# Attention on 128, 128 and 69 rows, angles computed once, both layer norms in one chain: one change to a fused vision-text layer on Trainium2

## What is computed

```python
h = tokens(x) @ W + b + pos          # 1 class token + 196 patches of 3x14x14
h = concatenate([h, txt], axis=1)    # 197 + 128 = 325 rows
xn = layernorm(h)
kp, qp = tanh(xn @ Wk + bk) * pi, tanh(xn @ Wq + bq) * pi     # 4 sets x 8 planes = 32 columns each
V = xn @ Wv + bv
total = sum_s w_s * Re(cumsum(exp(i kp_s) * V) * conj(exp(i qp_s)))   # causal, no softmax
pos = sigmoid(pw) * the same with fixed position angles
g = sigmoid(xn @ Wg + bg)
h = h + xn + (g * total + (1 - g) * pos) / sqrt(8 * position) @ Wo + bo
x2 = layernorm(h)
scores = sigmoid(x2 @ gate.T); top 2 of 64 experts, at most 256 rows each
h = h + shared_ffn(x2) + routed_experts(x2)
```

## Time and profile before

| | us |
|---|---|
| three runs, median (lowest to highest) | 1717.03 (1716.64 to 1719.13) |
| the profiled execution, its own time | 1715.9 |
| its span, first to last instruction | 1714.0 |
| PE busy (share) | 1519.8 (89%) |
| DVE busy | 1470.9 (86%) |
| POOL busy | 1273.1 (74%) |
| ACT busy | 1187.7 (69%) |

### The profile page before, as it was taken

The page is one execution under the profiler, slowest core; times in us unless marked ns, Lnnn a source line. Parts: engine busy times, 40 slices in busy tenths (PEclk is TensorE's granted clock), DMA queues, the critical chain, the costliest instruction groups (busy, mean ns, idle before and its releaser), DMA issues.

```text
span 1714.0 us, 31340 instructions
## 1 busy us (share of the span) xinstructions
PE 1519.8 (89%) x9222; PEld 1169.7 (68%) x9222; DVE 1470.9 (86%) x6005; ACT 1187.7 (69%) x1997; POOL 1273.1 (74%) x1162
## 2 busy tenths in 40 slices
PE   2699999999999999999999999999999981776661
PEld 1477777777777777777777777777777760555551
DVE  2489999999999999999999999999999982886671
ACT  2898888888888888888888888888888740111110
POOL 0018777777777777787777777777777776688888
PEclk9899999999999999999999999999999986898885
DMA  8886666666666666665656566555555111576653
GB/s 132 216 218 140 142 140 137 132 131 124 124 118 120 112 119 112 113 111 110 110 110 111 113 112 110 112 113 113 114 113 111 42 25 45 99 114 89 101 78 34
DMA packets 259939, 193.51 MB, mean 113 GB/s; under 512 B 65514, under 2 KB 239269, under 8 KB 259785
## 3 DMA queue, kind: packets, MB, share of 16 engines
q1 hardware_dynamic: 206008, 173.23, 49.7%
q0 software_dynamic: 51200, 17.87, 8.7%
q10 hardware_dynamic: 2576, 0.60, 0.3%
HBM read 84.34 MB, written 83.73 MB: 98 GB/s over the span
## 4 chain that ended last, share of the span: by engine, by line
PE 72%; POOL 15%; issue 6%; ACT 3%; DVE 2%; DMA 1%; ACTq 1%; SPq 0%; POOLq 0%
PE bank L855 11%; POOL out_rows L602 10%; PE bank L915 8%; PE bank L932 8%; PE bank L1002 5%; PE bank L879 4%; PE bank L1010 4%; PE bank L892 4%; PE bank L863 4%; POOL slot_rows L561 3%; PE bank L974 3%; PE bank L969 2%; PE bank L964 2%; PE bank L986 2%; PE bank L953 2%
## 5 line engine op out<-in xcount | busy, mean ns | idle before, releaser
L561 POOL DMA_INDIRECT slot_rows<-xs,slot x768 | 869.3, 1132 | 241.2 <-issue 240.9
L619 ACT ACTIVATE img<-img 84x980 f32<-84x980 f32 (+1 forms) x192 | 342.2, 1784 | 17.5 <-DVE wcol L1203 13.1
L855 PE MATMUL bank<-img,w_tok 126*128 126x392 f32 (+1 forms) x640 | 224.2, 497 | 11.1 <-DMA img<-img 11.0
L602 POOL DMA_INDIRECT out_rows<-img,etok x128 | 199.5, 1559 | 30.0 <-issue 29.2
L855 PEld LDWEIGHTS bank<-img,w_tok 126*128 126x128 f32 (+1 forms) x640 | 122.9, 192 | 95.2 <-issue 14.7
L688 ACT ACTIVATE xs<-h,nb,rs 128x128 f32<-128x128 f32 x384 | 154.7, 482 | 18.4 <-DVE nb L1257 11.2
L915 PE MATMUL bank<-pos_a,v 128*128 128x325 f32 (+2 forms) x768 | 158.7, 355 | 1.3 <-ACT gt L758 1.3
L701 ACT ACTIVATE xh<-h,nb,rs 128x128 f32<-128x128 f32 x384 | 154.0, 482 | 1.0 <-DVE nb L1230 0.9
L932 PE MATMUL bank<-a_t,v 128*128 128x325 f32 (+2 forms) x768 | 152.0, 346 | 0.0
L539 POOL TENSOR_TENSOR rs<-ve,neg_half 128x6 f32<-128x6 f32 x64 | 87.3, 1365 | 81.2 <-DVE ve L1225 81.1
L915 PEld LDWEIGHTS bank<-pos_a,v 128*128 128x128 f32 (+1 forms) x768 | 125.1, 190 | 30.5 <-ACT gt L758 1.7
(11 more groups left out here) (203 smaller groups left out, 3711.0 us busy)
## 6 DMA issues: line engine op xcount, KB each, us to landing
img<-in_x SPq DMA_DIRECT2D x384, 150.1 KB
img<-img SPq DMA_DIRECT2D x256, 160.8 KB
img<-img SPq DMA_DIRECT2D x128, 128.6 KB
out_rows<-fin SPq DMA_DIRECT2D x128, 128.0 KB
slot_rows<-xs,slot POOLq DMA_INDIRECT x768
slot_rows<-init_rows SPq DMA_DIRECT2D x16, 540.0 KB, 9.5
img<-slot_rows SPq DMA_DIRECT2D x32, 270.0 KB
h<-in_txt SPq DMA_DIRECT2D x64, 128.0 KB, 2.2
```

What stands on the lines that cost most here:

```text
L561: g.indirect_dma_start(out=slots_d, out_offset=bass.IndirectOffsetOnAxis(ap=slot[0:nt, q.x, r, part:part + 1], axis=0), in_=xs[0:nt, q.x, ...
L602: g.indirect_dma_start(out=out, out_offset=bass.IndirectOffsetOnAxis(ap=etok[:, q.load, m:m + 1], axis=0), in_=ysum[:, q.load, m, :], in_o ...
L619: a.activation(cols[:, b0:b0 + nb, :], raw[:, q.u, :].rearrange("p (t b) -> p b t", b=P)[:, b0:b0 + nb, :], ACT.Copy)\
L855: ins = mm(bank[:, 7, 0:2 * PATCHES], w_tok[r, m, :], xk[r, k.u, :, m, :], start=(m == 0), stop=(m == SHIFT - 1))
```

## The change

It redraws the order of every engine's turn and changes four pieces of work.

- **Blocks.** The keys are cut at 128 and 256 instead of 128 and 197 (blocks of 128, 128 and 69 keys, the last from the rows of the third tile of values), so masks and products run over 325 + 197 + 69 = 591 columns a sample in place of 650. `mask` is two operations of 325 and 266 columns in place of one of 650.
- **Angles.** `wkq` has 64 distinct columns; both samples' angles go to one PSUM bank, side by side in its partitions, by two products of 325 columns. One tanh of 325 replaces two, the distance is made with two constants (one for keys, one for queries), and `weighted_queries` writes `qz` in one operation. What ACT moved across partitions is now moved by four DMAs of 32 x 325 on SP (`move_halves`), issued when ACT's `weighted_queries` is done, and `scores` waits for them.
- **One chain.** The statistics of the first norm of pair k and the second norm of pair k-2 lie side by side; one chain of 12 columns and one power on POOL (`rstd`) serve both.
- **Turns.** PE's and DVE's turns reach back to pair k-5, POOL's to k-6, ACT's to k-4, so PE has 69 turns in place of 67. SP spreads piece 1 of pair k+1 (not k+2) and loads pair k+3 (not k+4). During start-up four DMAs of 540 KB that clear `slot_rows` come between `spread_0` and `spread_1`.

The core of the diff (renamed buffers, banks and constants, the DVE body, and repeated forms are left out):

```diff
+BELOW = [L - i * TILE for i in range(NT)]
+BEGIN = [sum(BELOW[0:i]) for i in range(NT + 1)]
...
-    m1 = (p + TILE <= q1) & (p < T1)
-    q2 = np.arange(NIMG, L)[None, :]
-    m2 = p + NIMG <= q2
+    m1 = p + TILE <= q1
+    q2 = np.arange(2 * TILE, L)[None, :]
+    m2 = (p + NIMG <= q2) & (p + NIMG >= 2 * TILE)
...
+            def move_halves(q):
+
+                sp.wait_ge(S["a_qs"], q.count())
+                for s in range(2):
+                    lo, hi = slice(64 * s, 64 * s + 32), slice(64 * s + 32, 64 * s + 64)
+                    sp.dma_start(kq[hi, q.u, 0, :], qz[lo, q.u, 1, :]).then_inc(s_move[q.u], 16)
+                    sp.dma_start(qz[lo, q.u, 0, :], qz[hi, q.u, 1, :]).then_inc(s_move[q.u], 16)
...
             def body(k):
-                n4 = k.back(-4)
+                n3 = k.back(-3)
                 n2 = k.back(-2)
+                n1 = k.back(-1)
+                p1 = k.back(1)
                 p3 = k.back(3)
+                if p1.runs():
+                    move_halves(p1)
+                if n1.runs():
+                    spread_1(n1)
+                if n3.runs():
+                    if not first(n3):
+                        load(n3)
                 if p3.runs():
                     store(p3)
                 if n2.runs():
                     spread_2(n2)
                     text(n2)
                     spread_0(n2)
...
-                    spread_1(n2)
-                if n4.runs():
-                    if not first(n4):
-                        load(n4)
...
-            def rstd_1(q):
-
-                pool.wait_ge(S["v_ve1"], q.count())
-                g.tensor_tensor(out=rs1[:, q.u], in0=ve1[:, q.u], in1=neg_half[:, :], op=ALU.pow).then_inc(S["p_rs1"], 1)
-
-            def rstd_2(q):
-
-                pool.wait_ge(S["v_ve2"], q.count())
-                g.tensor_tensor(out=rs2[:, q.u], in0=ve2[:, q.u], in1=neg_half[:, :], op=ALU.pow).then_inc(S["p_rs2"], 1)
+            def rstd(q):
+
+                pool.wait_ge(S["v_ve"], q.count())
+                g.tensor_tensor(out=rs[:, q.u], in0=ve[:, q.u], in1=neg_half[:, :], op=ALU.pow).then_inc(S["p_rs"], 1)
...
+                p1 = k.back(1)
+                p5 = k.back(5)
+                p6 = k.back(6)
+                if p6.runs():
+                    scatter(p6, 4)
+                if p1.runs(BEHIND):
+                    rstd(p1)
+                if p6.runs():
+                    scatter(p6, 5)
+                if p5.runs():
+                    ready(p5)
+                    scatter(p5, 0)
+                    scatter(p5, 1)
+                    scatter(p5, 2)
+                    scatter(p5, 3)
+            steps(body, 1, 6)
...
-            def angles_0(k):
-
-                act.wait_ge(S["pe_k0"], k.count())
-                a.activation(ph_t[:, 0, :], bank[:, 2, 0:L], ACT.Tanh, bias=bkq[:, 0:1]).then_inc(S["a_th0"], 1)
-
-            def angles_1(k):
-
-                act.wait_ge(S["pe_k1"], k.count())
-                a.activation(ph_t[:, 1, :], bank[:, 3, 0:L], ACT.Tanh, bias=bkq[:, 1:2])
...
+            def angles(k):
+
+                act.wait_ge(S["pe_k"], k.count())
+                a.activation(ph_t[:, :], bank[:, 5, 0:L], ACT.Tanh, bias=bkq[:, :]).then_inc(S["a_th"], 1)
 
             def distance(k):
 
-                act.wait_ge(S["a_th0"], k.count())
-                a.activation(ph_a[:, :, :], ph_t[:, :, :], ACT.Abs, bias=cst("delta")).then_inc(S["a_abs"], 1)
+                act.wait_ge(S["a_th"], k.count())
+                for i in range(2):
+                    ins = a.activation(ph_a[:, i, :], ph_t[:, :], ACT.Abs, bias=cst("delta")[:, i:i + 1])
+                ins.then_inc(S["a_abs"], 1)
...
-            def moved_queries(k):
+            def weighted_queries(k):
 
                 act.wait_ge(S["a_sin"], k.count())
-                for s in range(2):
...
+                if p4.runs():
+                    score_parts(p4)
+                if p3.runs():
+                    columns_2(p3)
                 if p1.runs():
-                    moved_queries(p1)
+                    columns_1(p1)
                 if k.runs():
                     image_rows(k)
+                if p3.runs():
+                    logit_columns(p3)
                 if p1.runs():
+                    angles(p1)
+                    distance(p1)
+                    waves(p1)
+                    weighted_queries(p1)
                     gate(p1)
-                if p2.runs():
-                    normal_2(p2)
+                if p3.runs():
+                    logit_rows(p3)
+                if n2.runs():
+                    if not early(n2, 2):
+                        turn_columns_2(n2)
+                if p3.runs():
+                    shared_silu(p3)
                 if n2.runs():
                     if not early(n2, 0):
                         turn_columns_0(n2)
+                    if not early(n2, 1):
+                        turn_columns_1(n2)
                 if p2.runs():
-                    columns_2(p2)
+                    normal_2(p2)
                 if k.runs():
                     normal_1(k)
...
+                pe.wait_ge(S["a_g"], y.count())
+                wait_dma(pe, s_move, y, 4)
+                wait(pe, S["v_su"], y, 2)
                 for i, (t0, _) in enumerate(TILES):
                     for s in range(2):
                         r = slice(64 * s, 64 * s + 64)
-                        b = (6, 4)[s]
-                        dst = (bank[:, b, 0:L], bank[:, b + 1, 0:L - TILE], bank[:, b + 1, L - TILE:L])[i]
-                        ins = mm(dst, kq[r, y.u, s, t0:t0 + TILE], qs[r, y.u, t0:L], start=(i < 2), stop=(i != 1),
+                        b = (3, 5)[s]
+                        at = 0 if i < 2 else BELOW[1]
+                        dst = bank[:, b + (i > 0), at:at + BELOW[i]]
+                        ins = mm(dst, kq[r, y.u, 0, t0:t0 + TILE], qz[r, y.u, 0, i * TILE:L], start=(i < 2), stop=(i != 1),
...
+                for i in range(NT):
+                    ins = mm(bank[:, s, i * TILE:L], v[:, y.u, s, i, :], pos_a[:, BEGIN[i]:BEGIN[i + 1]],
...
+            def angles(k):
 
                 pe.wait_ge(S["a_xt"], k.count())
-                mm(bank[:, 3, 0:L], wkq[:, 1, :], x_t[:, 1, :], start=True, stop=True).then_inc(S["pe_k1"], 1)
-
-            def angles_0(k):
-
-                mm(bank[:, 2, 0:L], wkq[:, 0, :], x_t[:, 0, :], start=True, stop=True).then_inc(S["pe_k0"], 1)
+                wait(pe, S["v_u"], k, 1)
+                for s in range(2):
+                    ins = mm(bank[64 * s:64 * s + 64, 5, 0:L], wkq[:, :], x_t[:, s, :], start=True, stop=True)
+                ins.then_inc(S["pe_k"], 1)
...
+                p4 = k.back(4)
+                p5 = k.back(5)
+                if p5.runs():
+                    counts(p5)
+                if p2.runs():
+                    values(p2)
+                if p4.runs():
+                    shared_1a(p4)
+                    shared_1b(p4)
+                    shared_3a(p4)
+                    shared_3b(p4)
+                if p2.runs():
+                    position_out_0(p2)
+                    position_out_1(p2)
+                    scores(p2)
                 if k.runs():
                     token(k)
                     if first(k):
                         position_products()
                 if p3.runs():
-                    shared_3a(p3)
-                    shared_3b(p3)
+                    transpose_2(p3)
+                if p2.runs():
+                    phase_out_1(p2)
+                    phase_out_0(p2)
                 if p1.runs():
-                    values(p1)
+                    transpose_1(p1)
                 if k.runs():
                     token_rows(k)
+                if p4.runs():
+                    shared_out(p4)
+                if p3.runs():
+                    logits(p3)
+                if p1.runs():
+                    angles(p1)
+                if p2.runs():
+                    project(p2)
                 if p1.runs():
                     gates(p1)
                 if p3.runs():
-                    shared_out(p3)
-                if p1.runs():
-                    scores(p1)
-                    position_out_1(p1)
-                    position_out_0(p1)
-                if p2.runs():
-                    transpose_2(p2)
-                if p1.runs():
-                    phase_out_0(p1)
-                    phase_out_1(p1)
-                if p3.runs():
-                    counts(p3)
-                if p2.runs():
-                    shared_1a(p2)
-                    logits(p2)
-                    shared_1b(p2)
-                if k.runs():
-                    transpose_1(k)
-                if p1.runs():
-                    project(p1)
-                if p2.runs():
-                    logit_rows(p2)
-            steps(body, 0, 3)
+                    logit_rows(p3)
+            steps(body, 0, 5)
...
```

(23 more changed lines are left out.)

422 lines of the change are left out of this document (166 added, 256 removed).

## The result

The changed kernel takes 1958.32 us (median of four runs, 1940.37 to 1963.12) against 1717.17 before: a ratio of 1.138, 95% interval 1.135 to 1.140. Slower, as predicted, but by 241 us and not 121; it lies outside the range of 1708 to 1860. The profiled execution took 1963.12 us, its span is 1960.9.

The account below looks back on a forecast made before the run. PE's work bounded the kernel before at 21.00 us a turn; after the change a ring through SP's queue would set 22.7. 1715.9 + 100 for 59 turns + 22 at the end = 1838 us, range 1708 to 1860.

Parts of the forecast that it names:

- SP's ring: Waits from one spread_1 landing through ACT, PE, DVE and SP's queue to the next: 22.7 us a turn.
- landing: Time from the end of the spread's issue until it has landed: 2.6 us, with 1.8 and 2.8 kept as bounds.
- The moves: Four SBUF-to-SBUF DMAs on SP: 0.78 us each, like spreads, between bounds 0.40 and 0.79; 3.1 us with gap.
- PE's need: PE's work in a turn after 620 columns, 1.04 us, are removed: 19.96 us.
- PE's cost is columns: PE's products priced at 1.68 ns a column, from token's 3.29 us for 5 x 392 columns.
- POOL's power: POOL's remaining power, with doubled columns: 2.54 us, between 1.37 and 2.74; POOL then needs 20.1 us a turn.
- Start and end: Start-up to token of pair 4: nothing, within 10 us; POOL's last five pairs at the end: 22 us more.
- PE's terms in the ring: transpose_2 through shared_out, including 0.17 until its last product is out and signal 0.05: 5.13 us.
- 59 x (22.7 - 21.0) = 100: Pairs 4 to 63: 59 turns lengthen from 21.0 to 22.7 us each, 100 us in all.
- The clock rival: PE's clock falls to 1.2 GHz each turn, doubling its 5.1 us: turn 27.8, time 2139 us; chance 0.04.
- cheap moves: Moves issue in 0.40 us each: ring 21.2, 1750 us; with landing 1.8, ring 20.5, 1708 us; chance 0.22.
- the ring doesn't close: Ring under 20.1 us, so PE and POOL set the turn: 0.9 us less a turn, 1685 us; chance 0.14.

Follow-up runs that it names:

- two scatters: Changed kernel with POOL issuing only two of a pair's 12 scatters (part 0), so most routed rows never reach the experts: 1815.4 us.
- both edits: Changed kernel with the store and the four moves both issued behind spread_1 in SP's queue: 1701.43 us, ratio 0.990 to the kernel before.
- the reordered kernels: Changed kernel with SP's store behind the next spread_1: 1714.49 us; with the four moves behind spread_1 as well: 1701.43 us.
- both edits and a pause ahead of `token`: Kernel with store and moves behind spread_1, plus a PE wait for normal_2 ahead of token: 2071.49 us.
- scatters out of the stretch: Changed kernel with one POOL wait added: six of a pair's 12 scatters wait for add_shared of the turn: 2037.36 us.
- before, with the new blocks: Kernel before with only the keys cut at 128 and 256 (blocks of 128, 128 and 69): 1710.41 us, ratio 0.996.
- opened ring: Changed kernel with the store moved in SP's queue from ahead of spread_2 to behind the next spread_1: 1714.49 us, ratio to before 0.999.
- moves behind: Changed kernel with the four moves issued behind spread_1 on SP, store where it was: 1799.23 us.
- six: Changed kernel with six of a pair's 12 scatters, so half of the routed rows never reach the experts: 1862.21 us.
- pause filled: Changed kernel with four unused products of 325 columns added on PE ahead of token: 1865.5 us.
- pause ahead of `scores`: Changed kernel with PE waiting for spread_1 ahead of scores and not ahead of token: 2020.24 us.

## Why the prediction was right, and where it was wrong

- **SP's ring sets the turn: right.** The store behind the spreads gives back all of it. Its terms, in the turn above: ACT 4.2 (4.26 predicted), PE 5.3 (5.13), DVE 1.0 (1.0), SP from the store's start to the end of `spread_1`'s issue 9.3 (9.65), landing 3.2 (2.6). Sum 22.9 against 22.7, and 22.65 with two scatters.
- **The moves: 0.78 us was too much.** They take 0.56 to 0.59, 2.45 us for four. They are SBUF to SBUF like the spreads, which take 0.79; the kind of transfer doesn't fix the price. It lies inside the bounds, and the landing, 3.2 us after the issue ended, lies outside them (1.8 to 2.8); the two misses nearly cancel, and that the sum fits so well is luck to this extent. The text's landing rose as well, from 2.2 to 3.1 us; the spreads and moves now stand right behind it, but whether they are the cause wasn't tested. By the section of the Trainium skill that the prediction weighed (DMA: Bandwidth & Descriptors, Anatomy of one DMA) the estimate for the spread's landing was 1.65 us, further off than the rows; that section is on DMAs issued by POOL, and the spreads are issued by SP.
- **PE's need: wrong in the step "PE's cost is columns".** 118 columns in a group gave 0.05 us, not 0.20. The angles gave 0.45 of 0.55 (0.72 us recorded for both samples, 0.65 to the next group, against 2 x 0.55). So PE needs about 20.3 us (the turn with both edits), not 19.96. In the changed kernel PE idles and this costs nothing; it is why the fast version gains 1% and not the 2% of 1685 us.
- **POOL's power: 2.30 us, predicted 2.54** (bounds 1.37 and 2.74).
- **Start and end: nearly right.** Start 5 us (nothing, within 10). End 19 us (22); POOL again decides it: the experts' first rows are fetched 111.7 us after the last `token` (1700.43 less 1588.73), before 91.6.
- **What failed: PE's terms in the ring.** The step "59 x (22.7 - 21.0) = 100" took PE's part of the ring for its recorded durations and "signal 0.05", and put the clock at nothing. The ring itself brought 1.92 x 58 = 111 us. But from the recorded end of `shared_out` to `add_shared` it took 1.68 us on average and not 0.05, which is 95 us, and the clock brought 14 more. No row of before shows a late signal, so the range had no room for what an idle PE does to its own work. Why the signals are late stays open.
- **The clock rival** was priced for every turn at 5.1 us. It came in 15 of 58 turns, at 0.8 in all but one, since only `token` was slow, and half of the 1.7 us that it lost was covered by the wait for ACT behind it. What the Trainium skill says (TensorE: Matmul & The Clock Gate, HAM oscillation), that products between waits for DMAs start at the slow clock, holds in kind: clock 1.00 without a pause, 0.97 with short ones, 0.90 with one of 2.8 us. But not in every turn, and with two scatters much the same pauses left it at 1.00.
- **The rivals "cheap moves" and "the ring doesn't close"** are refuted for the changed kernel; the second is what the reordered kernels do. There the gain was 0.68 us a turn, against the 0.9 that the rival gave: 39 us in 58 turns, of which start (6) and end (19) take 25.

## What to carry to other kernels

When a change alters where a DMA stands in SP's queue, follow the waits of one whole turn through every queue until they come back to their start; if that ring is longer than the busiest engine's work, it sets the turn, and moving three DMAs behind the others can be worth 12% of a kernel. Don't take products by their columns where they are narrower than their weights. And treat a small new pause of a full PE as a risk of its own: price it by what the work behind it does afterwards, not by its length, and compare the semaphore updates with the recorded ends; if the pause can't be removed, a few products that nobody needs may be cheaper than the pause.

## What was not expected of the hardware

PE's semaphore updates can come microseconds after the recorded end of the products. Of the updates that the traces hold for the turns, so many came more than 0.1 us after the recorded end:

| kernel | late, of PE's updates | longest, us |
|---|---|---|
| before | 0 of 1085 | 0.03 |
| changed (three profiles, the last with other semaphore numbers) | 300 of 815, 308 of 828, 350 of 836 | 4.6 |
| both edits and a pause ahead of `token` | 318 of 872 | 6.3 |
| scatters out of the stretch | 185 of 759 | 5.3 |
| before, with the new blocks | 140 of 742 | 1.3 |
| opened ring; moves behind; both; two scatters; six; pause filled; pause ahead of `scores` | 0 of 1052 to 1073 each | 0.03 |

It is PE alone: in the profiles of the first five rows (of the changed kernel the first one) no update of DVE, ACT or POOL came more than 0.02 us late.

At least in part it is the signals that are late, and not the products that are slower than recorded. In the turn shown above, `shared_out` (L877) is followed by the logits (L966). The two that wait for them start 0.06 us apart, though the logits' products alone take 0.70:

```profile
722.48 0.77 PE L966 MATMUL bank<-x_t,gate_t 128*64 128x325 f32 x4
```

```profile
726.55 0.96 DVE L1275 TENSOR_TENSOR fin<-bank,h 128x768 f32<-128x768 f32 x1 [3.93 <-remote]
726.61 0.44 ACT L714 ACTIVATE lg_t<-bank 128x325 f32<-128x325 f32 x1 [0.97 <-remote]
```

With the scatters moved, the updates of `values` and `shared_1b` come 0.06 us apart in all 57 turns, with 1.1 us of products between their recorded ends. The updates are held back and then move in a row. In the changed kernel this is so in 16 of the 38 turns in which the signal of `shared_out` was over 1 us late; in the others the two updates are further apart, and there the trace doesn't tell the two apart.

What brings it about is known in part. In the changed kernel, and in the one with both edits and a pause, PE paused 1.3 to 2.3 us a turn ahead of `token`, and twelve indirect DMAs of POOL ran beside what followed. Taking away the pause, ten of the scatters or six of them ended it, and so did a pause ahead of `scores` instead; putting the pause back brought it back. But it isn't a rule that both are needed: with the scatters moved the signals were late without a pause ahead of `token`, and with the new blocks they were late, if by little, without any pause. Scatters were there in every case, and in the four turns of the changed kernel with the longest waits `add_shared` started 0.7 to 1.0 us after POOL's last scatter of a batch. No run has all twelve scatters away, and what holds PE's signals back stays open.
